# Two-layer graph network: self weights applied to rows sorted by type through DRAM, and a window pass without branches

## What is computed

```
h = relu(layernorm(x))
xr = einsum('nd,rde->rne', h, W_rel)            # 3 edge types
agg = segment_sum(xr[edge_type, src] + b_rel[edge_type], dst, 625)
xs = einsum('nd,tde->tne', h, W_self)           # 3 node types
h_self = xs[node_type, arange(625)] + b_self[node_type]
x = x + relu(h_self + agg)
```

## Time and profile before

| | us |
|---|---|
| median of 3 runs | 350.64 (350.07 to 350.78) |
| the profiled execution, its own time | 351.21 |
| its span | 349.40 |
| PE busy | 310.5 (89% of the span) |
| DVE busy | 213.7 (61%) |
| ACT busy | 143.0 (41%) |
| POOL busy | 70.0 (20%) |

### The profile page before, as it was taken

The page is one execution under the profiler, slowest core; times in us unless marked ns, Lnnn a source line. Parts: engine busy times, 40 slices in busy tenths (PEclk is TensorE's granted clock), DMA queues, the critical chain, the costliest instruction groups (busy, mean ns, idle before and its releaser), DMA issues.

```text
span 349.4 us, 5835 instructions
## 1 busy us (share of the span) xinstructions
PE 310.5 (89%) x2113; PEld 247.3 (71%) x2113; DVE 213.7 (61%) x546; ACT 143.0 (41%) x276; POOL 70.0 (20%) x92
## 2 busy tenths in 40 slices
PE   3527449998999999999989999999899999999994
PEld 2104326766777777886878878999788888888883
DVE  5685994789994333343343695387685647574721
ACT  1009311151311333225234254367786655564621
POOL 4002350063250320337000141041000101010101
PEclk9999686999999999999999999999999999999999
DMA  5702311003021030000361000000000000000000
GB/s 166 240 1 60 123 63 58 2 1 120 3 83 40 3 122 2 2 3 2 120 190 52 1 0 2 0 2 0 1 3 2 2 30 2 32 2 32 2 32 27
DMA packets 7324, 14.19 MB, mean 41 GB/s; under 512 B 630, under 2 KB 646, under 8 KB 7290
## 3 DMA queue, kind: packets, MB, share of 16 engines
q1 hardware_dynamic: 6836, 13.13, 11.1%
q10 hardware_dynamic: 454, 0.61, 0.6%
HBM read 12.46 MB, written 1.28 MB: 39 GB/s over the span
## 4 chain that ended last, share of the span: by engine, by line
PE 74%; DVE 14%; ACT 4%; issue 3%; DMA 2%; DVEq 1%; POOL 0%; ACTq 0%
PE banks L1135 23%; PE banks L1081 8%; PE banks L1121 8%; PE banks L1215 7%; PE banks L1201 6%; PE banks L1190 6%; PE banks L1235 4%; PE banks L990 4%; DVE key_hot L725 3%; DVE row_hot L724 3%; DMA raw<-in_L_gnn_W_qkv_dram 2%; PE banks L1225 1%; PE banks L1111 1%; PE banks L1098 1%; PE banks L1067 1%
## 5 line engine op out<-in xcount | busy, mean ns | idle before, releaser
L389 POOL TENSOR_TENSOR w_hl<-raw,w_hl 128x512 fp32r<-128x512 f32 x24 | 30.6, 1298 | 88.4 <-ACT w_hl L457 88.4
L1135 PE MATMUL banks<-w_hl,hT 128*128 128x512 f32 x180 | 48.0, 418 | 0.0
L913 DVE CUSTOM_DVE_ANT_0 s_sb<-banks,mask_add 128x640 f32<-128x640 f32 x40 | 32.6, 821 | 22.1 <-PE banks L1190 22.0
L725 DVE TENSOR_SCALAR key_hot<-iota,picked 128x480 f16<-128x480 f16 x100 | 41.6, 416 | 0.0
L1135 PEld LDWEIGHTS banks<-w_hl,hT 128*128 128x128 f32 x180 | 35.2, 202 | 8.5 <-issue 0.2
L990 PE MATMUL banks<-key_hot,row_hot 128*128 128x480 f16 x100 | 28.4, 421 | 14.2 <-DVEq L755 14.0
L596 ACT ACTIVATE p_sb<-s_sb,neg_max 128x640 f32<-128x640 f32 x40 | 32.9, 823 | 17.3 <-DVE neg_max L913 17.3
L724 DVE TENSOR_SCALAR row_hot<-iota,picked 128x128 f16<-128x128 f16 x100 | 33.0, 330 | 6.5 <-issue 4.8
L1081 PE MATMUL banks<-adjT,h 128*128 128x320 f16 x240 | 33.8, 299 | 0.4 <-DVE zT_even L790 0.4
L466 ACT ACTIVATE adjT<-banks 128x480 f16<-128x480 f32 x20 | 11.3, 566 | 53.0 <-PE banks L1013 53.0
L1081 PEld LDWEIGHTS banks<-adjT,h 128*128 128x128 f16 x240 | 23.0, 98 | 10.5 <-issue 1.0
(11 more groups left out here) (160 smaller groups left out, 481.2 us busy)
## 6 DMA issues: line engine op xcount, KB each, us to landing
raw<-in_L_gnn_W_self_dram SPq DMA_DIRECT2D x3, 1024.0 KB, 5.8
raw<-in_L_gnn_W_rel_dram SPq DMA_DIRECT2D x3, 1024.0 KB, 5.2
raw<-in_L_gnn_W_qkv_dram SPq DMA_DIRECT2D x3, 1024.0 KB, 5.3
xs<-in_x_dram SPq DMA_DIRECT2D x1, 1024.0 KB
raw<-in_L_gnn_W_ff_dram SPq DMA_DIRECT2D x1, 1024.0 KB, 5.5
out_dram<-ybuf SPq DMA_DIRECT2D x4, 256.0 KB, 2.0
bv_rows<-in_L_gnn_b_qkv_dram ACTq DMA_DIRECT2D x1, 256.0 KB
bff_rows<-in_L_gnn_b_ff_dram ACTq DMA_DIRECT2D x1, 256.0 KB
```

What stands on the lines that cost most here:

```text
L389: nc.gpsimd.tensor_tensor(w_hl[q % 2][:, 1, kt], raw[q % 2][:, kt], w_hl[q % 2][:, 0, kt].bitcast(F32), ALU.subtract).then_inc(s_wlo, 1)
L725: return nc.vector.tensor_scalar(to_key, iota[:], float(KEYS * w), key, ALU.add, ALU.is_equal)
L913: nc.vector.tensor_tensor_reduce(s_sb[:, n % NS, :].rearrange("p (a j) -> p a j", a=2), banks[:, c:c + 2, 0:HALF], mask_add[:, it, :].rear ...
L1135: ins = mm(to, lhs[:, pl, kt, it * P:(it + 1) * P], weights[:, pw, kt, c0:c0 + cn], start=(start and n == 0), stop=(n == 3 * KD - 1), skip ...
```

## The change

The self product no longer runs over all three types. Each node gets a place in an order sorted by type, where each type starts at a tile of 128; with three types that makes at most seven tiles. The places are computed on the chip (PE ranks, DVE sums). POOL scatters the five tiles of `in0` row by row to a DRAM buffer, which ACT's queue has filled with zeros before; SP loads seven tiles back; each is transposed (unit `turn`) and meets the weights of its own type in plain float32, four matmuls of 512 columns (unit `self`), with the offset into the weights from a register. ACT copies both results out of PSUM. SP stores seven tiles to a second DRAM buffer, and POOL gathers five tiles from it into `self_sum`. The self weights are no longer split; ACT splits the first two relational weights when the last of these 14 units is done. They use banks 2 to 4 and stand in windows 6 to 12.

G is 6. The pass has no branch per window: only if some window touches more than six chunks is every window of a half redone, in one block. The bank is freed by ACT's store instead of DVE's residual nop. Statistics of the rows are moved on DVE from window 0 to before group 1. POOL's splitting of `h16` moves from window 8 to behind the scatters.

The diff's parts stand in this order: the lists, then SP, POOL, ACT, DVE and PE.

```diff
-    G, F = 5, 3
+    G, F = 6, 1
+    PIPE_AT, PIPE_STEP = 6, 1
+    SORTED = NT + T - 1
...
-        side[2] = [("hT", 0, 0), ("hT", 1, 0)]
-        for it in range(2, NT):
-            side[it + 1].append(("hT", it, 0))
-        for n in range(T * NT):
-            side[5 + n].append(("self", n // NT, n % NT))
...
+        pipe = [("turn", 0), ("turn", 1)]
+        for t in range(SORTED):
+            pipe += [("self", t)] + [("turn", t + 2)] * (t + 2 < SORTED)
+        for n, u in enumerate(pipe):
+            pipe_side[PIPE_AT + max(n - 1, 0) * PIPE_STEP // 2].append(u)
...
+            self_weights(0)
+            sp.wait_ge(s_scat, 16 * NT)
+            for half, (t0, t1) in enumerate(((0, 2), (2, SORTED))):
+                sp.dma_start(hs[:, t0:t1, :], sorted_d[t0 * P:t1 * P, :].rearrange("(t p) d -> p t d", p=P)
+                             ).then_inc(s_hs[half], 16)
+            self_weights(1)
+            self_weights(2)
+            for q in range(R + 4):
+                if q == 2:
+                    for t in range(SORTED):
+                        sp.wait_ge(s_pcopy, pipe_no[("self", t)] + 1)
+                        sp.dma_start(self_d[t * P:(t + 1) * P, :], hs[:, t, :]).then_inc(s_kept, 16)
...
+            pool.wait_ge(s_place, 1)
+            pool.wait_ge(s_zero, 16)
+            for it in range(NT):
+                pool.wait_ge(s_y0, it + 1)
+                nc.gpsimd.indirect_dma_start(sorted_d, bass.IndirectOffsetOnAxis(ap=place_u[:, it:it + 1], axis=0),
+                                             in0[:, it, :], None).then_inc(s_scat, 16)
+            for it in range(NT):
+                pool.wait_ge(s_h16hi, it + 1)
+                nc.gpsimd.tensor_tensor(h16[:, 1, it, :], in0[:, it, :], h16[:, 0, it, :], ALU.subtract
+                                        ).then_inc(s_h16lo, 1)
             for kt in range(KD):
-                weights_lo(4, kt)
+                weights_lo(0, kt)
+            pool.wait_ge(s_kept, 16 * SORTED)
+            for it in range(NT):
+                nc.gpsimd.indirect_dma_start(self_sum[:, it, :], None, self_d,
+                                             bass.IndirectOffsetOnAxis(ap=place_u[:, it:it + 1], axis=0)
+                                             ).then_inc(s_self, 16)
+            for kt in range(KD):
+                weights_lo(1, kt)
...
             def store_window(w):
-                act.wait_ge(s_win, w + 1)
+                act.wait_ge(s_slot, G * (w + 1))
+            act.wait_ge(s_x, 48)
+            act.dma_start(sorted_d.rearrange("(t p) d -> p t d", p=P),
+                          zero_rows[:].unsqueeze(1).broadcast_to([P, SORTED, D])).then_inc(s_zero, 16)
...
                 if w >= 1:
+                    for u in pipe_side[w - 1]:
+                        pipe_copy(u)
+                        if u == pipe[-1]:
+                            weights_hi(0)
+                            weights_hi(1)
                     for u in side[w - 1]:
                         unit_part(u)
                     store_window(w)
...
+            node_types()
             hot_group(0)
+            type_masks()
...
+            sorted_places()
+            factors(0, 0, NT)
+            hot_group(1)
+            tile_types()
             window_bounds()
-            hot_group(1)
             chunk_keys()
...
-                further_groups(w)
+                if w == 3:
+                    widest = dve.value_load(bounds[0:1, 2, NW:NW + 1], min_val=1, max_val=EC)
+                if w + 1 in stored:
+                    all_groups(stored.index(w + 1))
                 if w < NW - 2:
                     hot_group(w + 2)
-                residual(w)
...
             def first_chunks(w):
                 if w >= 2:
-                    pe.wait_ge(s_res, w - 1)
+                    pe.wait_ge(s_adj, w - 1)
+            def pipe_unit(u):
+                    pe.wait_ge(s_hs[0 if t < 2 else 1], 16)
+                    for kt in range(KD):
+                        ins = nc.tensor.transpose(pipe_bank(u)[:, kt * P:(kt + 1) * P], hs[:, t, kt * P:(kt + 1) * P],
+                                                  ident[:])
...
+                    for kt in range(KD):
+                        ins = mm(pipe_bank(u), hsT[:, t % 4, kt, :], w_self[:, bass.ds(offsets[t] + kt * D, D)],
+                                 start=(kt == 0), stop=(kt == KD - 1))
```

More of the change, by code:

```diff
@@ L493, in unit_part @@
                 kind = u[0]
-                if kind not in ("hT", "z", "wt", "h2T", "q", "k"):
+                if kind not in ("z", "wt", "h2T", "q", "k"):
                     return
                 act.wait_ge(s_unit, number[u] + 1)
[L497 to L501, removed]
+                if kind == "h2T":
                     it = u[1]
@@ L993, in _ @@
             first_chunks(0)
-            pe.wait_ge(s_keys, BOUNDS)
-            pe.wait_ge(s_fill, 18)
-            _, counts = nc.values_load_multi_w_load_instructions(
-                bounds[0:1, 2, 0:NW + 1], engines=(pe.engine,), min_val=0, max_val=EC,
-                skip_runtime_bounds_check_because="the vector engine clamped them")
-            widest = counts[NW]
-            def window(w):
-                if w:
-                    first_chunks(w)
-                with pe.If(counts[w] > G):
-                    with pe.Fori(G, counts[w], F):
-                        pe.wait_ge(s_further, pe.snap(filled, min_val=1, max_val=1 << 20))
-                        pe.reg_add(filled, filled, F)
-                        for k in range(F):
-                            mm(banks[:, w % 2, 0:KEYS], further_row[:, k, :], further_key[:, k, :],
-                               start=False, stop=True, skip_group_check=True).then_inc(s_taken, 1)
-                mm(banks[:, w % 2, 500:501], ident16[:], ident16[:, 0:1], start=False, stop=True,
-                   skip_group_check=True).then_inc(s_win, 1)
+            pe.wait_ge(s_type, 1 + T)
@@ new lines, in _ @@
+            pe.wait_ge(s_fill, FILLS)
+            mm(banks[:, 4, 420:420 + NT * T], below[:], type_mask[:].rearrange("p n t -> p (n t)"), start=True,
+               stop=True, skip_group_check=True)
+            for it in range(NT):
+                ins = mm(banks[:, 4, 420 + (it + 1) * T:420 + (NT + 1) * T].rearrange("p (n t) -> p n t", t=T), ones[:],
+                         type_mask[:, it:it + 1, :].broadcast_to([P, NT - it, T]),
+                         start=False, stop=True, skip_group_check=True)
@@ new lines, in _, with all_chunks @@
+            ins.then_inc(s_prep, 1)
+            def all_chunks(half):
+                with pe.If(widest > G):
+                    pe.wait_ge(s_adj, stored[half])
+                    for w in range(half * NW // 2, (half + 1) * NW // 2):
+                        count = pe.value_load(bounds[0:1, 2, w:w + 1], min_val=1, max_val=EC)
+                        if w >= 2:
+                            pe.wait_ge(s_stored, w - 1)
+                        mm(banks[:, w % 2, 500:501], ident16[:], ident16[:, 0:1], start=True, stop=True,
+                           skip_group_check=True)
+                        with pe.Fori(0, count, F):
+                            pe.wait_ge(s_further, pe.snap(filled, min_val=1, max_val=1 << 20))
+                            pe.reg_add(filled, filled, F)
+                            for k in range(F):
+                                mm(banks[:, w % 2, 0:KEYS], further_row[:, k, :], further_key[:, k, :],
+                                   start=False, stop=True, skip_group_check=True).then_inc(s_taken, 1)
+                        mm(banks[:, w % 2, 500:501], ident16[:], ident16[:, 0:1], start=False, stop=True,
+                           skip_group_check=True).then_inc(s_again, 1)
@@ L1140, in _ @@
             for w in range(NW):
-                window(w)
+                if w:
+                    first_chunks(w)
+                if w == 2:
+                    pe.wait_ge(s_keys, EDGE_KEYS)
+                    pe.wait_ge(s_place, 2)
+                    widest = pe.value_load(bounds[0:1, 2, NW:NW + 1], min_val=1, max_val=EC)
+                    _, offsets = nc.values_load_multi_w_load_instructions(
+                        tile_off_i[0:1, 0:SORTED], engines=(pe.engine,), min_val=0, max_val=(T - 1) * KD * D,
+                        skip_runtime_bounds_check_because="the vector engine worked them out")
+                if w + 1 in stored:
+                    all_chunks(stored.index(w + 1))
+                for u in pipe_side[w]:
+                    pipe_unit(u)
                 for u in side[w]:
                     unit(u)
-                if w == 1:
-                    pe.wait_ge(s_keys, NODE_TYPES)
-                    nc.tensor.transpose(banks[:, 4, 400:400 + NT], ntype_f[:], ident[0:NT, 0:NT]).then_inc(s_prep, 1)
                 if w == 6:
                     pe.wait_ge(s_bias, BIASES_IN)
-                    nc.tensor.transpose(banks[:, 3, 176:176 + 3 * KD], bqkv_r[:], ident[0:3 * KD, 0:3 * KD]
```

(1 more changed line is left out.)

303 lines of the change are left out of this document (179 added, 124 removed).

## The result

| us | before | after |
|---|---|---|
| median | 350.71 (350.07 to 351.20, 4 runs) | 337.23 (336.00 to 337.87, 4 runs) |
| span of the profiled execution | 349.40 | 335.1 |
| pass over | 118.6 | 105.0 |
| from there to the end | 230.8 | 230.1 |

The ratio is 0.9612, interval [0.9579, 0.9645]: faster by 13.5 us where 11.1 were forecast, and inside the range. Of the 14.3 us that the span lost, 13.6 lie in the pass.

The account below looks back on a forecast made before the run. The old pass was taken as DVE-bound to some 54 us, then PE-bound. New: start 43, PE-bound middle to 81.4, DVE-bound tail to 107.5 instead of 118.6, 230.8 carried over: span 338.3, median 339.5 us; range 325 to 350.

Parts of the forecast that it names:

- PE's float32 unit: Self product on PE, windows 6 to 12: seven units at 3.5 us each, 24.5 us in all.
- what lies behind the pass: Everything behind 118.6 us in the old kernel keeps its instructions and is carried over as 230.8 us.
- rival 2: Middle of the pass: float32 units cost only 1.9 to 2.0 us, 10.5 us less, time 329; chance 0.12.
- The clock in the middle: Windows 6 to 12: PE's clock falls after a partly idle front; 2.3 us added once.
- the two splits: Tail, windows 13 to 19: POOL's low parts of both weights hold up DVE, costing 2 x 4.2 = 8.4 us.
- Rival 3: Tail: contention of POOL with DVE is small, 4 to 9 us less, time 331 to 335; chance 0.17.
- the front: Up to the first float32 unit: DVE-bound, with the start of the float32 units at 43 us.
- the DRAM round trip is hidden by about 6 us of cover: Front: scatters end by 32, sorted rows are back at 37 us, before the start at 43.
- `h16` beside the one-hots: Front: POOL's five h16 pieces, 6.2 us, fall in DVE's stretch and cost it 5.2 us.
- rival 1: Front: scatters starve until DVE pauses near 41 us; start 52, time 348.5 or worse; chance 0.10 together with rival 4.
- Rival 5: Tail: half-idle PE's clock falls, up to 4 us more, 343; counted inside the forecast's 0.47.
- Rival 4: Pass: a window touches seven chunks or more, chunks are redone, 100 us in all, time above 430; chance 1%.

Follow-up runs that it names:

- Experiment 4: The changed kernel with the seven sorted self units in the reduced form of float32, their low bits left out; 321.96 us in a single execution.
- experiment 3: The changed kernel with POOL's eight low parts of the first two relational weights moved behind DVE's last one-hot; 329.41 us, ratio 0.9387.
- experiment 7: The changed kernel with POOL's low parts behind DVE's last one-hot and ACT's high-part splits moved to windows 16 and 18; 329.61 us, the profiled execution 335.49.
- experiment 6: The changed kernel with the DRAM buffer's zero fill started at 6 us, ahead of the load of x; 336.27 us, ratio 0.9593, one execution of 752.97 left out.
- experiments 2: The changed kernel with one more indirect DMA, an unused gather of rows of x, early on POOL; 336.38 us, ratio 0.9585.
- experiment 9: The kernel joining five moves of POOL, ACT, DVE and zero fill (326.54 us), with turns and float32 units from window 4 instead of 6; 329.76 us.

## Why the prediction was right, and where it was not

**Right for the reason given.** PE's float32 unit was forecast at 3.5 us from the full-width transposes and took 3.44; the chunks of a window 1.2 and took 1.22; what lies behind the pass 230.8 and took 230.1. The low estimate of 1.9 us (rival 2) is out. One float32 matmul of 512 columns took 3.44/4 = 0.86 us, where one in the reduced form had taken 2.83/12 = 0.24: 3.6 times. Experiment 4 gives 3.44 against 0.92 for the same unit, 3.7 times. The four passes that the Trainium skill gives for true float32 ("FP8 and Floating Point Precision", section TensorE Precision Notes) lie just above what the trace shows.

The clock in the middle fell once, as forecast. It was granted at 0.71 from 40.7 to 47.2 us, which is a mean: read in steps of one us it is 0.50 (1.2 GHz) from 38 to 44 us and 1.00 (2.4 GHz) from 45 on. PE had done nothing from 34.0 to 40.7. The first unit took 4.53 instead of 3.44 and the eight turn matmuls 1.97 instead of 2 x 0.44: 2.2 us, against 2.3 added.

The tail is DVE-bound through POOL, as the sum had it: the two splits were priced at 8.4 us, and taking them away brought 7.8 (experiment 3). Rival 3, that it would be small, is out. ACT's splits were named as second in line, and are (experiment 7).

**Right number, wrong reason: the front.** The step that failed reads "So the DRAM round trip is hidden by about 6 us of cover". The start was 40.7, close to the 43 forecast, but the forecast had DVE set it, with 5.2 us for `h16` beside the one-hots, and the rows back at 37. Instead PE waited 6.7 us for the rows. The scatters were free to go at 20.8 (25 had been allowed for the zero fill), but the five took 14.3 us and not 6.5, because one was starved (7.87 us where 1.3 was put). They were done at 35.1 and not at 32. The landing was sized rightly: 1.8 us from the end of the last scatter, for 2.0. The load took 3.8 us for 3. That makes 40.7 for 37. DVE's one-hots had let PE through window 6's chunks by 34.0, where 42 was forecast: its 6.2 us beside `h16` came later and fell into PE's wait. Two errors cancelled, a round trip too short by 3.7 us and a DVE stage too long by 8. The row on which the starvation could be read was there; it was used for rival 1 and left out of the forecast.

The price of `h16` itself was nearly right: in experiment 6 it cost DVE 5.9 us where 5.2 was put. In experiments 2, 4 and 6 the rows came 1.9 to 3.7 us earlier, the `h16` pieces came earlier too and held DVE where it was needed, and the start was 40.4, 40.2 and 40.3: there DVE set it, as forecast. So the stall moved the start by only 0.4 us (40.7 for 40.3), because this second bound stands close behind it. It is paid in full where the rows come later still, as in experiment 7's profiled execution.

**Rival 1 came in part.** It had all five scatters wait until DVE pauses. The Trainium skill, "SBUF — State Buffer", section "SBUF: two separate sides", says that GpSimd cannot write descriptors while DVE holds the port pair. The traces agree in direction (0.96 us with DVE idle, up to 8.33 beside it, and DMA engines that move nothing meanwhile), but they show one to three of five scatters hit and the rest at 0.96 to 1.40 us beside the same one-hots. So the start did not move to 52, as the rival had it. One scatter did just what the rival says: the last long one of experiment 7 came out when DVE paused, at 39.8 us for the 41 of the rival.

**Rival 5 came in part** too: in the tail PE was busy for 4.07 of 10.8 us, and behind that the clock was granted at 0.55 from 88.4 to 92.6, and the count unit took 3.78 us instead of 2.04. That is 1.7 us of the tail, which was 27.4 long against 26.1 forecast. Rival 4 is out: the trace has 120 chunk matmuls, six for each window, and none was redone.

**The sum.** Start 40.7 for 43 (2.3 less), middle 36.9 for 38.4 (1.5 less: seven turns of 0.44 for 0.63 are 1.3 of it), tail 27.4 for 26.1 (1.3 more), behind the pass 0.7 less. Together 3.2 us under the forecast span of 338.3.

What stays open: what lets some scatters through beside the one-hots and not others, and why the first stall ended between 28.7 and 29.7 us in all seven traces that have one.

## What to carry to other kernels

When a product with masks is replaced by one over sorted rows, count what leaves the vector engine as well as what leaves the matrix engine: in the kernel with the pass alone, DVE's masks stood on the chain. Keep POOL's work on tiles and its indirect DMAs apart in time from a dense train of short float16 operations on DVE: put them where PE is the bound, and let DVE pause for scatters that something waits for. And moving a unit forward helps only until the engine that feeds the stage behind loses its head start (experiment 9).

## What was not expected of the hardware

DVE and POOL shut each other out unevenly. In the kernel before, each one-hot beside a split took 1.25 to 1.41 us; here a single one took 6.23 us, through five POOL instructions in a row, and in the tail only `row_hot` was stretched (to 1.3 us, once to 3.69) while `key_hot` kept its 0.33 beside the split (DVE of the kernel after, in order of time):

```profile
83.07 1.28 DVE L828 TENSOR_SCALAR row_hot<-iota,picked 128x128 f16<-128x128 f16 x1
84.27 0.33 DVE L829 TENSOR_SCALAR key_hot<-iota,picked 128x480 f16<-128x480 f16 x1
84.52 1.28 DVE L828 TENSOR_SCALAR row_hot<-iota,picked 128x128 f16<-128x128 f16 x1
```

In the other direction one indirect DMA on POOL stood through 7.87 us of one-hots, some 37 of them at 0.42 us a pair. A scatter of 128 rows of 2 KB costs POOL 0.96 us undisturbed, its data land 2.7 to 3.0 us after the issue, and the first one of a kernel is no dearer (1.19 us).
